# A Mamba-style mixer on one core: the cross term joins the skip term on GpSimd, and its matmul moves between the halves of the output projection

## The reference

```python
zxBCdt = x @ in_proj_w.T                      # z 512, xc 512, dt 8 (one per head), B 64, C 64
dt = softplus(Bm + dt_bias)
xc = silu(depthwise_causal_conv(xc, conv_w, conv_b))      # 4 taps in time
xh = xc.reshape(B_sz, L, N_HEADS, HEAD_DIM)               # 8 heads of 64
a_bar = exp(dt * -exp(A_log))
def step(h, t):                                           # a scan over the 256 tokens
    a_t, b_t, c_t, x_t = t
    h = a_t[:, :, None, None] * h + b_t[:, None, None, :] * x_t[..., None]
    return h, einsum('bhdn,bn->bhd', h, c_t)
y = ys + xh * D_param[None, None, :, None]                # the skip term
y = rms_norm(y.reshape(B_sz, L, D_INNER) * silu(z), norm_w)
x = layernorm(x + y @ out_proj_w.T)
```

## Time and profile before

| | us |
|---|---|
| median of 3 runs (2431.63 to 2433.71) | 2431.78 |
| the profiled execution, its own time | 2424.99 |
| span of its records | 2423.2 |
| mixer, from the start to the last `a_x_t` | about 788 |
| one turn of the mixer in the loop | 23.44 |

### The profile page before, as it was taken

How to read it: one execution, slowest core, us unless ns; L and a number is a source line. 1 busy time by engine, 2 the same in 40 slices (tenths; PEclk the granted TensorE clock), 3 DMA queues, 4 the chain that set the end, 5 groups by cost and what they waited for, 6 DMA issues and landing times. The chain is left out here.

```text
span 2423.2 us, 53605 instructions
## 1 busy us (share of the span) xinstructions
PE 2191.4 (90%) x15804; PEld 1910.5 (79%) x15805; DVE 1790.1 (74%) x4428; ACT 1396.7 (58%) x3046; POOL 1258.2 (52%) x1411
## 2 busy tenths in 40 slices
PE   6999999999997897999999999999958999999776
PEld 5777777777775786888888888888848999999733
DVE  7888888888886424676777777677746777777778
ACT  5565565655653424666666666666626665556533
POOL 4677676776765001343434344343435776667755
PEclk9999999999998898999999999999979999999955
DMA  4011011110100453222222222222246877777588
GB/s 146 27 31 39 26 39 35 30 39 26 39 30 22 164 201 101 80 93 84 94 77 82 91 78 82 79 95 77 75 156 203 254 242 220 242 226 238 174 291 269
DMA packets 185263, 278.49 MB, mean 115 GB/s; under 512 B 26076, under 2 KB 107492, under 8 KB 185188
## 3 DMA queue, kind: packets, MB, share of 16 engines
q1 hardware_dynamic: 171140, 240.84, 31.8%
q0 software_dynamic: 12960, 35.67, 4.1%
q10 hardware_dynamic: 1088, 1.07, 0.1%
HBM read 184.13 MB, written 93.38 MB: 115 GB/s over the span
## 5 line engine op out<-in xcount | busy, mean ns | idle before, releaser
L1439 ACT ACTIVATE b_wk_f<-b_ps_s,b_nmx 128x77 f32<-128x77 f32 x1024 | 234.6, 347 | 15.4 <-DVE b_nmx L1487 15.4
L570 DVE SCALAR_TENSOR_TENSOR a_conv<-a_xc_pad,a_cw,a_conv 128x256 f32<-128x256 f32 x384 | 237.2, 677 | 8.4 <-ACT a_conv L457 8.4
L1447 ACT ACTIVATE b_pT<-b_ps_pT 77x1024 f32<-77x1024 f32 x128 | 130.7, 1021 | 142.3 <-PE b_ps_pT L1345 142.3
L2054 POOL DMA_INDIRECT made_scratch<-c_o_s,c_to x142 | 147.8, 1041 | 86.4 <-issue 42.4
L112 PE MATMUL c_ps_h<-c_xT_hi,c_w 128*128 128x256 f32 x568 | 168.0, 296 | 26.6 <-DMA c_b_c<-in_c_b 20.6
L1926 ACT ACTIVATE c_hid<-c_ps_h,c_b_c 128x256 f32<-128x256 f32 x284 | 111.6, 476 | 134.4 <-issue 76.0
L1503 DVE TENSOR_TENSOR b_oT_lo<-b_ps_oT,b_oT_hi 128x512 fp32r<-128x512 f32 x128 | 88.0, 687 | 130.6 <-ACT b_oT_hi L1453 130.6
L1732 POOL CAST w<-b_w_raw 128x256 f32 (+1 forms) x32 | 13.6, 425 | 323.9 <-DMA b_w_raw<-in_c_w 323.9
L1430 ACT ACTIVATE b_qT<-b_ps_q,b_bq_s 128x256 f32<-128x256 f32 x256 | 107.7, 473 | 112.4 <-PE b_ps_q L114 109.6
L1970 DVE TENSOR_TENSOR c_h_lo<-c_hid,c_h_hi 128x1024 fp32r<-128x1024 f32 x71 | 97.5, 1373 | 91.5 <-ACT c_h_hi L1935 60.9
L112 PE MATMUL c_ps_o<-w,c_h_hi 128*128 x568 | 160.0, 282 | 3.5 <-DVE c_h_lo L1970 3.5
(11 more groups left out here) (271 smaller groups left out, 7858.8 us busy)
## 6 DMA issues: line engine op xcount, KB each, us to landing
c_w<-parts_scratch SPq DMA_DIRECT2D x71, 1024.0 KB
c_xa<-sent_scratch SPq DMA_DIRECT2D x71, 260.0 KB, 2.9
d_got<-made_scratch SPq DMA_DIRECT2D x32, 512.0 KB, 5.4
keys_scratch<-k_k_s SPq DMA_DIRECT2D x8, 1232.0 KB, 4.8
b_kz<-keys_scratch SPq DMA_DIRECT2D x64, 154.0 KB, 2.8
b_vv<-values_scratch SPq DMA_DIRECT2D x32, 308.0 KB
a_xT_f<-in_xT SPq DMA_DIRECT2D x32, 256.0 KB, 3.1
a_x_f<-in_x SPq DMA_DIRECT2D x32, 256.0 KB, 2.7
```

What stands on the lines that cost most here:

```text
L570: dve.scalar_tensor_tensor(out=conv[:, m, :], in0=xc_pad[:, m, k:k + L], scalar=cw[:, m, k:k + 1], in1=conv[:, m, :], op0=ALU.mult, op1=AL ...
L1439: last = act.activation(pe_[:, u.par, c, :], s_scores[:, c // (C // GM), c % (C // GM), :], ACT.Exp, bias=nmx[:, u.par, c:c + 1])
L1447: act.activation(pT[:, u.par, :, :], ps_pT[0:LK, :, :], ACT.Copy).then_inc(s_pTc, 1)
L2054: pool.indirect_dma_start(routing.made, bass.IndirectOffsetOnAxis(to[:, t.slot, c:c + 1], 0), o_s[:, t.par, c, :], None).then_inc(s_sent[t ...
```

## The change

Three stages move and one addition changes place. On GpSimd, `scale_x` makes the skip term of half 1 into a new tile `x1d` and then adds `off_r` to it to give `xd[1]`; `join` loses the addition `t2`. On VectorE, `off_r` becomes a stage of its own (`scale_off`) ahead of the last taps, and `add_d` goes ahead of `normalise`. On TensorE, `out` is cut in two halves, with `mix_off` between them and `mix` behind both.

```diff
-            def out(b):
-                ...
-                for c in range(NT):
+            def out(c):
+                def run(b):
+                    if c == 0:
+                        ...
                     for m in range(MI):
                         last = split3(...)
-                last.then_inc(s_out, 1)
+                    last.then_inc(s_out, 1)
-                (decay(1), 1), (out, 2), (mix, 1), (mix_off, 1)])
+                (decay(1), 1), (out(0), 2), (mix_off, 1), (out(1), 2), (mix, 1)])
```

```diff
             def add_d(b):
-                dve.wait_ge(s_xd, b.count(1, 1))
                 for c in range(NT):
+                    dve.wait_ge(s_xd, b.count(NT, c + 1))
                     dve.wait_ge(s_Y, b.count(NT, c + 1))
                     ...
                     dve.tensor_tensor(t1[:, c, :], p01[:, c, :], xd[:, c, :], ALU.add).then_inc(s_t1, 1)
+
+            def scale_off(b):
                 dve.wait_ge(s_off, b.count(1, 1))
                 dve.wait_ge(s_rc, b.count(1, 1))
                 if not b.before(1):
-                    dve.wait_ge(s_t2, b.ago(1).count(1, 1))
+                    dve.wait_ge(s_xd, b.ago(1).count(NT, NT))
                 dve.tensor_tensor(off_r ...
-                (taps(1, 2), 0), (weigh(0), 1), (weigh(1), 1), (taps(2, 3), 0), (normalise, 3), (add_d, 1),
+                (taps(1, 2), 0), (weigh(0), 1), (weigh(1), 1), (scale_off, 1), (taps(2, 3), 0), (add_d, 1), (normalise, 3),
```

```diff
-                for c in range(NT):
-                    last = pool.tensor_tensor(xd[:, c, :] ..., x_t[:, c, :] ..., d_b ..., ALU.mult)
-                last.then_inc(s_xd, 1)
+                pool.tensor_tensor(x1d[:, :] ..., x_t[:, 1, :] ..., d_b ..., ALU.mult).then_inc(s_x1d, 1)
+                pool.tensor_tensor(xd[:, 0, :] ..., x_t[:, 0, :] ..., d_b ..., ALU.mult).then_inc(s_xd, 1)
+                pool.wait_ge(s_x1d, b.count(1, 1))
+                pool.wait_ge(s_or, b.count(1, 1))
+                pool.tensor_tensor(xd[:, 1, :], x1d[:, :], off_r[:, :], ALU.add).then_inc(s_xd, 1)
@@ join
                 pool.tensor_tensor(y[:, b.par, 0, :], t1[:, 0, :], zs[:, b.par, 0, :], ALU.mult).then_inc(s_y, 1)
-                pool.wait_ge(s_or, b.count(1, 1))
-                ...
-                pool.tensor_tensor(t2[:, :], t1[:, 1, :], off_r[:, :], ALU.add).then_inc(s_t2, 1)
-                pool.wait_ge(s_t2, b.count(1, 1))
-                pool.tensor_tensor(y[:, b.par, 1, :], t2[:, :], zs[:, b.par, 1, :], ALU.mult).then_inc(s_y, 1)
+                pool.wait_ge(s_t1, b.count(NT, NT))
+                pool.tensor_tensor(y[:, b.par, 1, :], t1[:, 1, :], zs[:, b.par, 1, :], ALU.mult).then_inc(s_y, 1)
```

More of the change, by code:

```diff
@@ L186, in mixer_phase @@
         off_r = sb("off_r", [P, DI])
-        t2 = sb("t2", [P, DI])
+        x1d = sb("x1d", [P, DI])
         y = sb("y", [P, 2, NT, DI])
@@ L236, in mixer_phase @@
                              "mv", "x1", "t1", "or"))
-        s_xlo, s_cx, s_xd, s_lm, s_t2, s_y, s_ri, s_ve, s_rs = (
-            sem(n) for n in ("xlo", "cx", "xd", "lm", "t2", "y", "ri", "ve", "rs"))
+        s_xlo, s_cx, s_xd, s_lm, s_x1d, s_y, s_ri, s_ve, s_rs = (
+            sem(n) for n in ("xlo", "cx", "xd", "lm", "x1d", "y", "ri", "ve", "rs"))
         N_LOADS = 8
@@ L419, in turn_y @@
                 last.then_inc(s_yT, 1)
-            def out(b):
-                if b.before(1):
-                    pe.wait_ge(s_wout, MI + 2)
-                pe.wait_ge(s_ylo, b.count(1, 1))
-                if b.known() and b.value() >= n_seq - 2:
-                    pe.wait_ge(s_res, b.ago(1).count(NT, NT))
-                else:
-                    pe.wait_ge(s_bcc, b.ago(-2).count(1, 1))
-                for c in range(NT):
+            def out(c):
+                def run(b):
+                    if c == 0:
+                        if b.before(1):
+                            pe.wait_ge(s_wout, MI + 2)
+                        pe.wait_ge(s_ylo, b.count(1, 1))
+                        if b.known() and b.value() >= n_seq - 2:
+                            pe.wait_ge(s_res, b.ago(1).count(NT, NT))
+                        else:
+                            pe.wait_ge(s_bcc, b.ago(-2).count(1, 1))
                     for m in range(MI):
@@ L432, in out @@
                                       pair(wo_hi, wo_lo, slice(None), m), m == 0, m == MI - 1)
-                last.then_inc(s_out, 1)
+                    last.then_inc(s_out, 1)
+                return run
             run_steps(pe, n_seq, [
                 (in_x, 0), (turn_y, 2), (in_z, 0), (in_bc, 0), (step_size, 0), (scores, 1), (decay(0), 1), (turn_x, 1),
-                (decay(1), 1), (out, 2), (mix, 1), (mix_off, 1)])
+                (decay(1), 1), (out(0), 2), (mix_off, 1), (out(1), 2), (mix, 1)])
         @block.scalar
@@ L481, in y_high @@
                 if not b.before(1):
-                    act.wait_ge(s_out, b.ago(1).count(1, 1))
+                    act.wait_ge(s_out, b.ago(1).count(NT, NT))
                 act.activation(yT_hi[:, :, :], ps_yT, ACT.Copy).then_inc(s_yhi, 1)
@@ L514, in take_x @@
                     act.wait_ge(s_Y, b.ago(1).count(NT, NT))
-                    act.wait_ge(s_xd, b.ago(1).count(1, 1))
+                    act.wait_ge(s_xd, b.ago(1).count(NT, 1))
                     act.wait_ge(s_cx, b.ago(1).count(1, 1))
@@ L642, in residual @@
             def residual(b):
-                dve.wait_ge(s_out, b.count(1, 1))
+                dve.wait_ge(s_out, b.count(NT, NT))
                 dve.wait_ge(s_ri, b.count(2, 2))
@@ L725, in scale_x @@
                     pool.wait_ge(s_t1, b.ago(1).count(NT, NT))
-                for c in range(NT):
-                    last = pool.tensor_tensor(xd[:, c, :].rearrange("p (h d) -> p h d", h=H),
-                                              x_t[:, c, :].rearrange("p (h d) -> p h d", h=H),
-                                              d_b[:, :].unsqueeze(2).to_broadcast([P, H, HD]), ALU.mult)
-                last.then_inc(s_xd, 1)
+                pool.tensor_tensor(x1d[:, :].rearrange("p (h d) -> p h d", h=H),
+                                   x_t[:, 1, :].rearrange("p (h d) -> p h d", h=H),
+                                   d_b[:, :].unsqueeze(2).to_broadcast([P, H, HD]), ALU.mult).then_inc(s_x1d, 1)
+                pool.tensor_tensor(xd[:, 0, :].rearrange("p (h d) -> p h d", h=H),
+                                   x_t[:, 0, :].rearrange("p (h d) -> p h d", h=H),
+                                   d_b[:, :].unsqueeze(2).to_broadcast([P, H, HD]), ALU.mult).then_inc(s_xd, 1)
+                pool.wait_ge(s_x1d, b.count(1, 1))
+                pool.wait_ge(s_or, b.count(1, 1))
+                pool.tensor_tensor(xd[:, 1, :], x1d[:, :], off_r[:, :], ALU.add).then_inc(s_xd, 1)
             def spread_l(b):
@@ L750, in join @@
                 pool.tensor_tensor(y[:, b.par, 0, :], t1[:, 0, :], zs[:, b.par, 0, :], ALU.mult).then_inc(s_y, 1)
-                pool.wait_ge(s_or, b.count(1, 1))
-                if not b.before(1):
-                    pool.wait_ge(s_y, b.ago(1).count(NT, NT))
-                pool.tensor_tensor(t2[:, :], t1[:, 1, :], off_r[:, :], ALU.add).then_inc(s_t2, 1)
-                pool.wait_ge(s_t2, b.count(1, 1))
-                pool.tensor_tensor(y[:, b.par, 1, :], t2[:, :], zs[:, b.par, 1, :], ALU.mult).then_inc(s_y, 1)
+                pool.wait_ge(s_t1, b.count(NT, NT))
+                pool.tensor_tensor(y[:, b.par, 1, :], t1[:, 1, :], zs[:, b.par, 1, :], ALU.mult).then_inc(s_y, 1)
             def inv_rms(b):
```

## The result

The changed kernel takes 2501.18 us (median of 4 runs, 2497.62 to 2511.04), the kernel before 2431.91 in the same comparison. The ratio is 1.029, with an interval of 1.026 to 1.032. The forecast was 2438, its range 2423 to 2450: the sign was its likelier one, the size is missed by 63 us, and the time lies outside the range.

A forecast was written before the change was run, and what follows sets the result against it. TensorE's 1.6 us wait at L418 for GpSimd's last `a_y`, with VectorE's chain into L375 only 0.15 us behind. Loop 13 x (1.19 - 0.51) = +8.8, drain -2.7, sum +6.1 on 2431.78: 2438, range 2423 to 2450.

The forecast's parts named there:

- likelier one: Sign of the whole change: slower at 0.43, against faster at 0.30 and within 0.2% at 0.27.
- In_x ends at about 424.4: the wait of 1.56 at L418 is gone.: At TensorE's transposes of `y`: the second `a_y` ends at 423.8, before in_x, so the 1.56 us wait goes.
- L411 costs 0.92 and starts 1.84 behind `out`: On TensorE: the cross term costs 0.92 us wherever it stands; between the halves it starts about 1.84 behind `out`'s start.
- What VectorE does then: On VectorE after `t1[1]`: `a_l_dt` starts at 425.3 or 425.7 instead of 424.62; the first spreading stays nearly even.
- without the branch the cast is 0.06 early and gets in: Cast `a_xT_hi` on VectorE: without the loop's branch it asks at 2.05 us, before the second spreading at 2.11.
- third rival: At the cast between the spreadings: it misses in every turn, 26 x 0.8 - 2.7 = +18 us, 2450; chance 0.12.
- turn A: Turn without the loop's branch: the cast gets in between the spreadings, L375 starts at 432.11, 0.51 us shorter.
- turn B: Turn with the loop's branch: cast behind the second spreading, fourth tap overtaken by `a_xT_lo`, L375 at 433.81, 1.19 us longer.
- `a_xT_lo` overtakes the fourth tap: On GpSimd, turn with a late cast: `a_xT_lo` asks inside the third tap, and the fourth waits some 1.1 us.

The follow-up runs named there:

- all three orders: The changed kernel with the load before the store, normalise before add_d and x_low behind inv_rms: 2447.81 us, ratio 1.007.
- three matmuls added: The changed kernel with loads ahead of the store, x_low behind inv_rms and three small matmuls ahead of the first L375: 2442.49 us, ratio 1.003.

## Why the prediction was wrong, step by step

- **"In_x ends at about 424.4: the wait of 1.56 at L418 is gone."** Right: no wait for `a_y` at L418.
- **L411 costs 0.92 and starts 1.84 behind `out`.** Right: L411 starts 1.82 behind `out` (428.67 to 430.49). With TensorE's order alone, where the wait at L418 isn't removed, a turn at full clock is 23.95 against 23.44, and that wait is 2.09 against 1.56.
- **What VectorE does then.** Right in each point: the second `normalise` waits for the second `a_y` (2.09 us for the two), `a_v_sp` is down to 0.16, `a_l_dt` starts 3.96 behind `t1[1]` (436.55 to 440.51; I had 3.7 to 4.1), the first spreading 0.25 behind it.
- **"without the branch the cast is 0.06 early and gets in".** This step failed. VectorE was free at 442.61, as forecast. But I followed the cast on VectorE's side only. Its load stands behind the store on SP's queue, the store waits for `normalise`, and the change moves `normalise` behind the two `t1`: the load is issued at 440.23 and the cast starts at 443.26. So the cast misses in every turn: my third rival, 0.12, though for another reason than its 0.06. I had written of turn A and turn B where there was only turn B. With the load ahead of the store and the clock held, turns A and B are there.
- **`a_xT_lo` overtakes the fourth tap.** Right, and shown to be the term that counts: with it behind `inv_rms` the wait for `a_yT_lo` is gone at full clock.
- **The clock.** The larger failure, and one that no step of the prediction had: the sum takes every matmul at the duration that it has in before, that is at a granted clock of 1.00. My turns hold a new wait of 1.05 or 2.75 us at L375, and I took the matmuls behind it at their old durations, a term of nothing without a reason. At full clock the third rival's 2450 is what six added matmuls measure, 2449.6, and the late `a_yT_lo` costs 0.67 us a turn where I had 0.8. That the two agree to within 1 us is luck, with single executions between 2434 and 2465; the size is not. The cast waits for the second spreading whether its load is late or not (it ends 0.28 us behind it in the changed kernel, where the load is late, and 0.29 with VectorE's order alone, where it isn't), so `a_yT_lo` is as late as in that rival. The clock adds 2.06 us a turn on top, three quarters of the loss.

What stays open: why the clock falls behind one short wait and not behind another. At L375, in the loop's alternating turns, it fell behind a wait of 0.38 and not of 0.21 us with all three orders; with three matmuls added, behind 0.69 and not 0.37; with six, not behind 0.88; with normalise back and no matmul added, behind some waits of 0.20. With VectorE's order alone it fell behind 9 of 13 waits of 1.48 us (100 to 740 us). At L418 it fell behind six of 25 waits of 2.09 us and never behind the 1.56 of the kernel before. So the length of the wait alone doesn't decide it, and the list gives no price for a wait in advance. Also left open is how the shares of the two halves (1.015 and 1.021) go together in 1.029. Both halves alone keep the wait at L418, which the whole change removes, so they can't be added. The part of the change on GpSimd, the addition moved up, was never run alone.
